# A selective-scan kernel: spreading B as three exact bf16 parts in one bf16 matmul, three more idle products at the start, and new slot tables

## What is computed

```python
xn = layernorm(x)
xz = rmsnorm(xn) * norm_w @ W_in                      # split into xi, z (256 each)
xc = silu(causal_conv(xi, 4 taps) + conv_b)
dt, Bm, Cm = split(xc @ W_x, [64, 80])                # rank 64, 16 states for B, 16 for C
dt = softplus(dt @ W_dt + b_dt)
h  = scan over time of  h = exp(dt * A) * h + (dt * xc) * Bm     # 256 channels x 16 states
y  = (sum over states of h * Cm + D_skip * xc) * silu(z)
s  = xn + y @ W_out
g  = silu(top-2 of 8 experts of xn: relu(xn @ W1 + b1) @ W2 + b2, weighted)
out = x + s * g
```

## Time and profile before

| | us |
|---|---|
| median of 3 runs | 296.18 (295.96 to 296.21) |
| profiled execution, own time | 296.01 |
| its span, first to last instruction | 294.2 |
| TensorE busy in it | 274.6 (93%) |
| VectorE busy | 264.6 (90%) |
| POOL busy | 235.0 (80%) |
| ScalarE busy | 228.8 (78%) |

### The profile page before, as it was taken

The page is one execution under the profiler, slowest core; times in us unless marked ns, Lnnn a source line. Parts: engine busy times, 40 slices in busy tenths (PEclk is TensorE's granted clock), DMA queues, the critical chain, the costliest instruction groups (busy, mean ns, idle before and its releaser), DMA issues. The chain is left out here.

```text
span 294.2 us, 4278 instructions
## 1 busy us (share of the span) xinstructions
PE 274.6 (93%) x1259; PEld 144.0 (49%) x1259; DVE 264.6 (90%) x317; ACT 228.8 (78%) x444; POOL 235.0 (80%) x180
## 2 busy tenths in 40 slices
PE   7999989699999999799999999689999999999992
PEld 3543434165656445245556644225564664556461
DVE  5768999829999998999999999779999999999993
ACT  1477895989888984999988983899868677887640
POOL 6407976648799995669988999588879998799994
PEclk9999999989999999999999999999999999999999
DMA  6938671032039008432272084041039770000002
GB/s 171 276 100 194 149 172 37 0 96 53 0 81 205 4 0 188 99 102 47 53 175 60 2 194 92 1 111 38 0 84 206 176 179 0 2 0 1 3 0 71
DMA packets 16246, 25.18 MB, mean 86 GB/s; under 512 B 4136, under 2 KB 9631, under 8 KB 16224
## 3 DMA queue, kind: packets, MB, share of 16 engines
q1 hardware_dynamic: 15602, 24.25, 35.3%
q0 software_dynamic: 192, 0.52, 0.8%
q10 hardware_dynamic: 430, 0.14, 0.2%
HBM read 8.00 MB, written 1.18 MB: 31 GB/s over the span
## 5 line engine op out<-in xcount | busy, mean ns | idle before, releaser
L400 POOL TENSOR_TENSOR hc<-hs,Ct 128x1024 f32<-128x1024 f32 x63 | 149.2, 2384 | 17.3 <-DVE hs L922 12.8
L922 DVE TENSOR_TENSOR_SCAN hs<-dec,pdbu 128x1024 f32<-128x1024 f32 x64 | 144.1, 2272 | 0.6 <-ACT dec L570 0.4
L570 ACT ACTIVATE dec<-rep,negA 128x512 f32<-128x512 f32 x126 | 85.5, 722 | 0.8 <-DMA rep<-dt_u 0.8
L908 DVE TENSOR_TENSOR pdbu<-rep,px 128x1024 f32<-128x1024 f32 x62 | 73.5, 1217 | 13.6 <-PE px L1118 12.4
L1161 PEld LDWEIGHTS px<-w,hT 128*128 128x128 f32 x512 | 62.1, 194 | 16.7 <-issue 8.7
L1155 PE MATMUL px<-xnT,w 128*128 128x512 f32 x128 | 64.7, 611 | 0.7 <-DVE pdbu L908 0.5
L1161 PE MATMUL px<-w,hT 128*128 128x128 f32 x512 | 63.9, 279 | 0.5 <-DVE pdbu L908 0.5
L703 ACT ACTIVATE hT<-px,cols 128x512 f32<-128x512 f32 x64 | 43.5, 690 | 9.2 <-PE px L1155 7.6
L516 POOL TENSOR_TENSOR acc<-acc,ysc 128x512 f32<-128x512 f32 x29 | 37.8, 1303 | 9.2 <-ACT ysc L692 8.9
L692 ACT ACTIVATE ysc<-px,score 128x128 f32<-128x128 f32 x116 | 33.1, 368 | 13.9 <-PE px L1161 13.7
L1155 PEld LDWEIGHTS px<-xnT,w 128*128 128x128 f32 x128 | 21.3, 189 | 29.8 <-issue 18.2
(11 more groups left out here) (162 smaller groups left out, 276.9 us busy)
## 6 DMA issues: line engine op xcount, KB each, us to landing
rep<-dt_u SPq DMA_DIRECT2D x116, 128.0 KB, 2.4
Ct<-c_rows SPq DMA_DIRECT2D x16, 256.0 KB, 4.5
w<-in_L_ffn_W SPq DMA_DIRECT2D x1, 1024.0 KB
out<-xn SPq DMA_DIRECT2D x4, 256.0 KB, 2.5
x_sb<-in_L_attn_x SPq DMA_DIRECT2D x1, 768.0 KB, 5.8
rep<-dt_u POOLq DMA_DIRECT2D x4, 128.0 KB, 3.7
win<-in_L_attn_W_in SPq DMA_DIRECT2D x1, 256.0 KB, 3.2
x_sb<-in_L_attn_x ACTq DMA_DIRECT2D x1, 128.0 KB, 2.5
```

The costliest lines, as they stand in the source:

```text
L400: eng.tensor_tensor(hc[:, n % HC_RING], hs[:, n % HS_RING], Ct[:, k % 2, j:j + 1, :].to_broadcast([P, 2, CH]), ALU.mult).then_inc(hc_last ...
L570: act.activation(dec[:, n % DEC_RING, i, :], rep[:, q, 0, :], ACT.Exp, scale=negA[:, q, j:j + 1])\
L908: dve.tensor_tensor(pdbu[:, at:at + 2, :], rep[:, 2 * pair:2 * pair + 2, 1, :], B[:, None, :].to_broadcast([P, 2, CH]), ALU.mult).then_inc ...
L922: dve.tensor_tensor_scan(hs[:, n % HS_RING].rearrange("p b t -> p (b t)"), dec[:, n % DEC_RING].rearrange("p b t -> p (b t)"), pdbu[:, at: ...
```

## The change

The job "B" is split. Jobs 0 to 3 (first half of the first chunk) stay as they are. From job 4 on, B is taken as the sum of three bf16 numbers, exact for fp32. SP now writes the rows of both B and C to DRAM (`bc_rows`). It reads B back folded, 16 rows of 512 as 128 rows of 64 (`fold_B`). POOL splits it in four steps on 128 x 64 (`split_B`: round to bf16, subtract, round, subtract). SP carries the three parts into 48 rows of 512 in `thirds` (`unfold_thirds`, three transfers). One bf16 matmul with a bf16 selector `tsel` of 48 rows, which holds each 0/1 column three times, then spreads and sums the parts in one. `tsel` is made on POOL once, behind `rest_roots`. `dtp` has one buffer for two: the dt drain of a chunk waits for the B(3) job and for the write of the chunk before to DRAM. `csel` moves into a ring buffer that is free at the start. `BUSY["row"]` goes from 3 to 6. All slot tables are new.

```diff
-    0: ["gl", "m1b", "z1", "z0"], 2: ["m1a"], 3: ["m0b"], 10: ["gs"], 11: ["gb"],
+    0: ["gl", "z0", "z1", "m1b"], 1: ["m1a"], 2: ["m0b"], 10: ["gs"], 11: ["gb"],
...
 TABLE = [{
-    3: ["tr"], 7: ["xc1"], 9: ["xc0", "z0", "z1"], 12: ["dt"], 13: ["y0", "tn", "v0"], 15: ["y1", "gl"], 16: ["m2a"],
-    17: ["m2b", "m3a", "v1"], 19: ["m3b", "y2", "m4b", "y3", "m4a", "m5b"], 24: ["m5a", "y4", "m6a"], 25: ["y5"],
-    26: ["m6b"], 29: ["y6", "m7b", "m7a"], 30: ["gs"], 32: ["y7", "gb"], 38: ["o"],
+    4: ["tr"], 7: ["xc0"], 9: ["xc1", "z1", "z0"], 11: ["dt"], 13: ["y0", "tn", "v0", "m2b"], 15: ["y1"],
+    16: ["gl", "m2a"], 17: ["v1", "m3b"], 18: ["m3a"], 19: ["y2", "m4b", "m4a"], 20: ["y3"], 21: ["m5b"],
+    23: ["m5a"], 24: ["y4"], 25: ["m6a", "y5", "m6b"], 27: ["m7b"], 29: ["y6", "gs", "m7a"], 32: ["gb", "y7"],
+    38: ["o"],
 }, {
...
-    "second": [1], "gate": [1, 1, 3, 3, 5, 5, 5, 5, 6, 7, 7, 8, 8, 8, 10], "gate_e": [0], "gate_p": [1, 7, 7],
+    "second": [1], "gate": [1, 2, 3, 3, 5, 5, 5, 5, 6, 6, 7, 8, 9, 9, 10], "gate_e": [0], "gate_p": [0, 8, 8],
+    "third": [12],
...
-BUSY = {"row": 3, "xc1": 2}
+BUSY = {"row": 6, "xc1": 2}
+THIRDS, PIECE = 3, CH * STATES // P
...
-        dtp = sb("dtp", [P, 2, CH])
+        dtp = sb("dtp", [P, CH])
+        Bt = sb("Bt", [P, PIECE])
+        split = sb("split", [P, THIRDS, PIECE], BF16)
+        thirds = sb("thirds", [P, 2, CH], BF16)
...
         sel = sb("sel", [P, QUADS, GROUP, GD])
+        tri = sb("tri", [P, STATES])
+        tsel = sb("tsel", [P, QUADS, GROUP, GD], BF16)
         rsel = sb("rsel", [P, GD])
-        csel = sb("csel", [P, 2, GROUP, GD])
...
+        csel = ysc[:, YSC_RING - 1, 0:2 * P].rearrange("p (q i d) -> p q i d", q=2, i=GROUP)
+        bc_rows = nc.dram_tensor("bc_rows", [CHUNKS, 2 * STATES, CH], F32, kind="Internal").ap()
...
             def repeat_C(k):
 
                 wait_emptied(sp, "dt", k)
-                sp.dma_start(c_rows[k], dtp[RANK + STATES:RANK + 2 * STATES, k % 2, :]).then_inc(c_out, 16)
+                sp.dma_start(bc_rows[k], dtp[RANK:RANK + 2 * STATES, :]).then_inc(c_out, 16)
                 sp.wait_ge(c_out, 16 * (k + 1))
                 if k >= 2:
                     sp.wait_ge(hc_done, PER_CHUNK * (k - 1))
                 for i in range(GROUP):
                     sp.dma_start(Ct[GD * i:GD * (i + 1), k % 2],
-                                 c_rows[k].rearrange("(j s) t -> s j t", s=GROUP)[i].partition_broadcast(GD))\
+                                 bc_rows[k, STATES:].rearrange("(j s) t -> s j t", s=GROUP)[i].partition_broadcast(GD))\
                         .then_inc(c_in[k % 2], 16)
 
...
+            def fold_B(k):
+
+                if k > 0:
+                    sp.wait_ge(third_done, k)
+                sp.dma_start(Bt[:, :], bc_rows[k, 0:STATES].rearrange("r (s t) -> (r s) t", t=PIECE)).then_inc(b_in, 16)
+
+            def unfold_thirds(k):
+
+                sp.wait_ge(third_done, k + 1)
+                if k >= 2:
+                    wait_filled(sp, "B", DB * QUADS * (k - 1) - 1)
+                for c in range(THIRDS):
+                    sp.dma_start(thirds[STATES * c:STATES * (c + 1), k % 2, :].rearrange("r (s t) -> r s t", t=PIECE),
+                                 split[:, c, :]).then_inc(third_in[k % 2], 16)
+
             for k in range(CHUNKS):
                 repeat_C(k)
+                if k > 0:
+                    fold_B(k)
+                    unfold_thirds(k)
                 for pair in range(PAIRS):
                     if (k, pair) != (0, 0):
                         repeat_dt_u(k, pair)
+                if k == 0:
+                    fold_B(k)
+                    unfold_thirds(k)
...
+
+            def third_selectors():
+
+                pool.tensor_tensor(tri[:, :], ident[:, 0:STATES], ident[:, STATES:2 * STATES], ALU.add).then_inc(third_set, 1)
+                pool.wait_ge(third_set, 1)
+                pool.tensor_tensor(tri[:, :], tri[:, :], ident[:, 2 * STATES:3 * STATES], ALU.add).then_inc(third_set, 1)
+                pool.wait_ge(third_set, 2)
+                for j in range(QUADS):
+                    pool.tensor_copy(tsel[:, j], tri[:, GROUP * j:GROUP * (j + 1), None].to_broadcast([P, GROUP, GD]))\
+                        .then_inc(third_set, 1)
+
+            def split_B(k):
+
+                pool.wait_ge(b_in, 16 * (k + 1))
+                if k > 0:
+                    pool.wait_ge(third_in[(k - 1) % 2], 16 * THIRDS * ((k - 1) // 2 + 1))
+                pool.tensor_copy(split[:, 0, :], Bt[:, :]).then_inc(third_step, 1)
+                pool.wait_ge(third_step, 3 * k + 1)
+                pool.tensor_tensor(Bt[:, :], Bt[:, :], split[:, 0, :], ALU.subtract).then_inc(third_step, 1)
+                pool.wait_ge(third_step, 3 * k + 2)
+                pool.tensor_copy(split[:, 1, :], Bt[:, :]).then_inc(third_step, 1)
+                pool.wait_ge(third_step, 3 * k + 3)
+                pool.tensor_tensor(split[:, 2, :], Bt[:, :], split[:, 1, :], ALU.subtract).then_inc(third_done, 1)
...
             rest_roots()
+            third_selectors()
...
                 for k, i in steps_at(n, "gate_p"):
                     (gate_probs, gate_shares, gate_scores)[i](k)
+                for k, _ in steps_at(n, "third"):
+                    split_B(k)
...
                 elif job == "dt":
-                    if k >= 2:
-                        act.wait_ge(c_out, 16 * (k - 1))
-                        wait_filled(act, "B", DB * QUADS * (k - 1) - 1)
-                    ins = act.activation(dtp[0:RANK + 2 * STATES, k % 2, :], src[0:RANK + 2 * STATES, :], ACT.Copy)
+                    if k > 0:
+                        act.wait_ge(c_out, 16 * k)
+                        wait_filled(act, "B", QUADS - 1)
+                    ins = act.activation(dtp[0:RANK + 2 * STATES, :], src[0:RANK + 2 * STATES, :], ACT.Copy)
...
-                elif job == "B":
+                elif job == "B" and k < QUADS:
                     if k == 0:
                         pe.wait_ge(selected, N_SELECTED)
-                    wait_emptied(pe, "dt", k // (DB * QUADS))
-                    last = pe.matmul(dst[:, :], sel[:, k % QUADS].rearrange("p s d -> p (s d)"),
-                                     dtp[:, k // (DB * QUADS) % 2, :], start=True, stop=True)
+                        wait_emptied(pe, "dt", 0)
+                    last = pe.matmul(dst[:, :], sel[:, k].rearrange("p s d -> p (s d)"), dtp[:, :], start=True, stop=True)
+                elif job == "B":
+                    chunk = k // (DB * QUADS)
+                    pe.wait_ge(third_set, 2 + QUADS)
+                    pe.wait_ge(third_in[chunk % 2], 16 * THIRDS * (chunk // 2 + 1))
+                    last = pe.matmul(dst[:, :], tsel[0:THIRDS * STATES, k % QUADS].rearrange("p s d -> p (s d)"),
+                                     thirds[0:THIRDS * STATES, chunk % 2, :], start=True, stop=True)
```

More of the change, by code:

```diff
@@ L80 @@
 }, {
-    "gate_y": [23, 36], "last_table": [33],
+    "gate_y": [23, 40], "last_table": [40],
 }]
 START = {
-    "second": [1], "gate": [1, 1, 3, 3, 5, 5, 5, 5, 6, 7, 7, 8, 8, 8, 10], "gate_e": [0], "gate_p": [1, 7, 7],
+    "second": [1], "gate": [1, 2, 3, 3, 5, 5, 5, 5, 6, 6, 7, 8, 9, 9, 10], "gate_e": [0], "gate_p": [0, 8, 8],
+    "third": [12],
 }
@@ L217, in mamba_moe @@
         ysc = sb("ysc", [P, YSC_RING, CH])
-        c_rows = nc.dram_tensor("c_rows", [CHUNKS, STATES, CH], F32, kind="Internal").ap()
+        csel = ysc[:, YSC_RING - 1, 0:2 * P].rearrange("p (q i d) -> p q i d", q=2, i=GROUP)
+        bc_rows = nc.dram_tensor("bc_rows", [CHUNKS, 2 * STATES, CH], F32, kind="Internal").ap()
         def banks(name, n):
@@ L246, in mamba_moe @@
         acc_added = sem("acc_added")
+        b_in, third_step, third_done = sem("b_in"), sem("third_step"), sem("third_done")
+        third_set, third_in = sem("third_set"), [sem(f"third_in{i}") for i in range(2)]
         c_out, c_in = sem("c_out"), [sem(f"c_in{i}") for i in range(2)]
@@ L764, in _ @@
             dve.memset(xrT[:, :, 0:PAD], 0.0).then_inc(setup, 1)
-            dve.memset(dtp[RANK + 2 * STATES:P, :, :], 0.0).then_inc(setup, 1)
+            dve.memset(dtp[RANK + 2 * STATES:P, :], 0.0).then_inc(setup, 1)
             dve.memset(wdt[RANK:P, :], 0.0).then_inc(setup, 1)
@@ L1105, in fill @@
                     pe.wait_ge(setup, N_SETUP)
-                    last = pe.matmul(dst[:, :], wdt[:, b * P:(b + 1) * P], dtp[:, k % 2, :], start=True, stop=True)
+                    last = pe.matmul(dst[:, :], wdt[:, b * P:(b + 1) * P], dtp[:, :], start=True, stop=True)
                 elif job == "gl":
```

18 lines of the change are left out of this document (9 added, 9 removed), and 22 rows, old and new, of the table TABLE.

## The result

The changed kernel took 294.21 us (median of 4 runs, 293.81 to 294.45) beside 296.07 for the kernel before on the same chips (median of 4, 295.69 to 296.21). The ratio is 0.9938, with a 95% interval of 0.9921 to 0.9955. The profiled execution of the changed kernel took 294.09 us with a span of 292.3; before it was 294.2, so 1.9 us went from the span.

The account below looks back on a forecast made before the run. VectorE was taken as the bound, so cheaper TensorE work returns only VectorE's waits. Gains of 4.5 us less costs of 1.2 us gave -3.3 us: 292.9 us against the median of 296.18, range 288.3 to 297.0.

Parts of the forecast that it names:

- three of its own signs: Half clock in at most one stretch, no wait over 0.5 us at second chunk's end, VectorE and TensorE not waiting for POOL.
- The idle products: At the start, three more idle products delay the tap spreading 1.0 us and xc1's silu 0.5 us: cost 0.5 us.
- gate_probs: First chunk: moved to slot 0, it puts both products by C behind gri; first reduce and what follows +0.5 us.
- The largest wait: VectorE's wait for B(4): m2b adds 0.86 us, cheaper B takes 0.64 off; +0.2 us, wait about 5.8 us.
- The bf16 matmul: B jobs 4 to 31 on TensorE: one instruction each, 0.64 us saved a job, 17.9 us of TensorE work.
- The new route: B's rows through DRAM, POOL's split and three transfers: parts there ahead of B(4), costed at nothing.
- What comes back: VectorE's waits at second and third chunk ends, small waits and projection shrink: 0.57 + 1.35 + 0.69 + 1.9 = 4.5 us gained.
- The rival of the falls: Less TensorE work brings three more clock falls ahead of awaited Bs, 1.7 us each: 298.0 us; chance 0.15.

Follow-up runs that it names:

- The hold run: The changed kernel with 12 idle products into dt's own bank ahead of dt in the second and third chunk; 292.25 us, ratio 0.9877.
- the run with the moved product: The kernel before with one VectorE product of dt and xc (third chunk) in slot 36 instead of 34, its memset in 40 instead of 35; 297.03 us.
- the run with three idle products a job: The changed kernel with three idle products of 128 columns ahead of each bf16 B job; 304.91 us, ratio 1.0338.

## Why the prediction held, and where its working failed

The direction and the range held, at 294.2 where 292.9 was forecast: -1.9 us where the sum said -3.3. By three of its own signs the working was nevertheless wrong. The granted clock was 0.5 in three stretches ahead of the end, not one; the wait at the second chunk's end was 1.80 us, not under 0.5; and POOL appears newly as what VectorE waits for (0.6 and 0.5 us). Step by step:

- **The idle products** were right. The tap spreading started at 4.87, 1.14 us later (1.0 forecast), and the silu of xc1 at 16.27, 0.52 later (0.5). The clock rose at 13.4 as before.
- **gate_probs** was wrong. It did put both products by C behind gri (POOL at 37.51, to 42.18), but the reduce takes the halves in turn and its first four MATMULs need only the first product; it took 1.18 us instead of 1.06 and started no later against the first scan (14.06 us behind it, 14.03 before). The term of 0.5 us was 0.1.
- **The largest wait** was 5.99 us where 5.8 was forecast. B(4) is read 8.22 us behind dt's start instead of 7.87: 0.35 us, of which m2b is 0.86 and the cheaper B takes back 0.54.
- **The bf16 matmul**: 28 of one MATMUL each. The one at 127.12 is followed at 127.44, 0.32 us behind, so a job saves 0.54 us and not 0.64, 15 us in all and not 17.9. The 216 ns that the forecast cites from the Trainium skill (TensorE: Matmul & The Clock Gate, "Back-to-back issue gap") were not seen here: no MATMUL followed a bf16 B by less than 0.315 us. It changes little.
- **The new route** was free, as costed: the first chunk's four split steps took 0.24 to 0.31 us each, from 55.45 to 56.77, single later ones up to 0.79, and no B waited for its parts.
- **What comes back** is the term that failed. It stood at 4.5 us. Apart from B(4), VectorE waited 7.5 us for the B jobs and the projection before; the forecast left 2.9 of it, and 6.7 stayed, so 0.8 us came back. At the second chunk's end the wait was to go and rose from 0.57 us to 1.80. At the third's, B(19)'s wait of 2.66 us went, as forecast, but B(20)'s stayed at 1.92 (2.18 before), and B(17)'s rose from 0.31 to 1.10. The projection's wait at 112.44 went too, but a new one of 1.64 stands at the next chunk's, at 179.85. The hold run shows what stood in its place: with the clock held, the first is 0.1 and B(20)'s 0.96, so that 3.9 us of waits are left and 3.5 come back. So the step that failed is the overlap: the forecast let the saved work shorten the waits in full and left out that TensorE, idle ahead of dt, would do dt at 1.2 GHz. The rest of the miss, B(17) and the projection, no run has explained.
- **The rival of the falls** is thus part of what happened: two more falls than in the profile before, not three. The forecast treated it as another case with a chance of 0.15, when it was a term of the sum. Its price per fall, 1.7 us, was the price in TensorE's time, and that is what dt shows (3.54 against 1.92); in VectorE's waits it was 1.8 and 1.0, and 1.0 each in the span. Rows 10 gave reason to cost it: 1.71 busy of 3.4 us was the nearest row to the case that fell, and the change cut work from just there. Trainium skill, TensorE: Matmul & The Clock Gate, "What's actually happening": activity releases the throttle, and its lack brings it back. These traces agree in the direction, with 0.83 and 0.66 us busy of 3.4 ahead of the falls and 3.40 of 3.4 ahead of none, but little work alone did not make a fall (last section).
- **What was not in the sum at all** is 3.0 us of VectorE's own time (products of dt and xc, correction, memset). Its idle time, start included, rose by 1.4 us. Part of the shorter operations had only covered waits, so the two can't simply be set against each other; but the forecast's sign was right partly by luck, for a reason it didn't have. Why the correction steps are shorter wasn't followed up; the eight products are told above.

## What to carry to other kernels

When work is taken off TensorE, look at each of its idle stretches and at what follows: if a short job there decides a wait, fill the stretch with products into the bank that this job will overwrite, which here cost nothing and gave 2 us. Making an engine's work cheaper is worth what its order can use; the same edit alone was worth nothing clear of the spread under the old order. When work is put back to test that, read from the trace how long it really takes: three idle products took 0.77 us where 0.65 was expected and 0.54 wanted. And before a long wait is blamed on the job that ends it, ask what the jobs behind that one need: moving B(4) only changed the name of the wait. Last, look at how two engines' operations fall against each other before a shorter busy time is put down to the edit: 2.2 us of it came from eight products, most of which no longer started under POOL's.

## What the runs showed of the hardware that was not expected

The clock's steps came at times that differ between executions (rise between 10.8 and 14.7 us). Idle stretches of the same length had different ends. The one of 2.60 us ahead of dt at the third chunk's end brought no fall in the kernel before (dt at 189.29) and one in the run with the moved product (dt at 189.61, fall at 190.8). Those of 2.76 and 2.85 us brought one each in the changed kernel, and none in the run with three idle products a job. There TensorE was even busy less ahead of dt, as its view of windows and its timeline show:

```profile
124.20:127.60 3.40, 0.66 (x8) 0.01 (x1) 3.40 (x3) 3.37 (x5) 1.09 (x2) 1.00 0.55 123
```

```profile
127.61 1.93 PE L1157 MATMUL px<-xc,wx 128*96 128x512 f32 x4 [2.76 <-ACT xc L643]
```

So neither the length of the stretch nor how little TensorE did in it settled whether the clock fell; the time at which it lay differed, and what about it decides, no run tells.

And a VectorE product of two 128 x 512 operands in SBUF, 0.66 to 0.72 us when clear of POOL, took the rest of a running elementwise operation of POOL plus 0.55 us when it started under one, up to 2.42 us. A POOL product that started during such a one took 2.81 us instead of 2.36.
